# The sixth dense pass of a graph network, written as short inner loops of six matmuls

## What is computed

```python
edge_index = jnp.stack([src, dst])
x = _layernorm(x + L0(x))   # three layers of: t = x @ W.T + b; x = (t + segment_sum(t[src], dst)) / 2
x = _layernorm(x + L1(x))   # h = x @ W; segment_sum(norm * h[src], dst) + b
x = _layernorm(x + L2(x))   # the same with a PReLU
x = _layernorm(x + L3(x))   # per edge: z = silu(bn(Wg @ [x_src, x_dst])), softmax weights, segment_sum
```

## Time and profile before

| | |
|---|---|
| median of 3 runs | 7904.57 us |
| span of the profiled execution | 7903.8 us |
| TensorE matmul busy | 5452.6 us (69%), 34773 matmuls |
| VectorE busy | 3716.0 us (47%) |
| GpSimd busy | 1922.7 us (24%) |
| ScalarE busy | 1419.9 us (18%) |
| DMA, mean over the span | 121 GB/s |
| mean granted TensorE clock | 0.825 of 2.4 GHz |

### The profile page before, as it was taken

The page is one execution under the profiler, slowest core; times in us unless marked ns, Lnnn a source line. Parts: engine busy times, 40 slices in busy tenths (PEclk is TensorE's granted clock), DMA queues, the critical chain, the costliest instruction groups (busy, mean ns, idle before and its releaser), DMA issues.

```text
span 7903.8 us, 132209 instructions
## 1 busy us (share of the span) xinstructions
PE 5452.6 (69%) x34773; PEld 3268.0 (41%) x34774; DVE 3716.0 (47%) x12527; ACT 1419.9 (18%) x4414; POOL 1922.7 (24%) x3005
## 2 busy tenths in 40 slices
PE   5999999869999999999321211111115899888883
PEld 1333333346666666666100000000002588877773
DVE  8888888733223444455100000000001488888887
ACT  0111233200000000000000000000000176665552
POOL 1222122100000000000577767777774000000000
PEclk8999999879999999999655555555556999999997
DMA  1000111135565656555433333333336555444442
GB/s 40 33 41 41 65 76 78 65 110 191 185 194 187 194 184 194 184 187 182 140 107 107 113 107 109 107 108 108 109 103 146 154 138 129 123 119 114 110 111 59
DMA packets 305154, 958.44 MB, mean 121 GB/s; under 512 B 55676, under 2 KB 124888, under 8 KB 285929
## 3 DMA queue, kind: packets, MB, share of 16 engines
q1 hardware_dynamic: 238729, 741.78, 30.4%
q0 software_dynamic: 66400, 216.36, 10.2%
HBM read 765.85 MB, written 192.08 MB: 121 GB/s over the span
## 4 chain that ended last, share of the span: by engine, by line
PE 48%; another core or an unknown queue 21%; DVE 13%; issue 12%; DVEq 2%; ACT 2%; SPq 1%; DMA 1%; ACTq 0%; POOLq 0%; POOL 0%; PEld 0%; PEldq 0%
PE banks L678 28%; PE banks L637 12%; DVE HSf L1028 3%; PE banks L632 2%; PE banks L627 2%; DVE HSf L1024 1%; DVE HSf L1035 1%; PE banks L668 1%; DVE HSf L1005 1%; PE banks L731 1%; ACT HSf L563 1%; PE banks L738 1%; DVE HSf L1030 1%; ACT AB L518 1%
## 5 line engine op out<-in xcount | busy, mean ns | idle before, releaser
L678 PE MATMUL banks<-HSf,AB 128*128 128x384 bf16 (+2 forms) x14406 | 2727.3, 338 | 1812.8 <-issue 1786.7
L678 PEld LDWEIGHTS banks<-HSf,AB 128*128 128x128 bf16 x14406 | 1417.4, 99 | 3012.7 <-issue 2160.9
L474 POOL DMA_INDIRECT HSf<-table_d,IX x1600 | 1515.0, 947 | 644.0 <-issue 488.6
L903 DVE TENSOR_REDUCE US<-banks 128x128 f32<-128x384 f32 (+1 forms) x294 | 164.1, 558 | 2977.4 <-remote 1738.4
L861 DVE TENSOR_SCALAR T<-T 128x784 bf16<-128x784 f16 x2352 | 985.1, 419 | 224.2 <-PE banks L637 208.1
L637 PE MATMUL banks<-T 128*128 128x392 bf16 x4704 | 965.6, 337 | 3.7 <-DVE T L862 3.0
L637 PEld LDWEIGHTS banks<-T 128*128 128x128 bf16 x4704 | 378.3, 99 | 565.0 <-DVE T L862 380.6
L862 DVE TENSOR_SCALAR T<-T 128x128 bf16<-128x128 f16 x2352 | 581.6, 247 | 0.0
L563 ACT ACTIVATE HSf<-HSf 128x130 f32<-128x130 f32 x1808 | 575.5, 392 | 0.5 <-DVE HSf L1039 0.5
L462 POOL DMA_DIRECT2D table_d<-T x1 | 2.5, 2545 | 2241.1 <-DVE HSf L879 2241.1
L518 ACT ACTIVATE AB<-banks 128x392 f32 x784 | 347.1, 494 | 1102.4 <-PE banks L641 1102.4
(11 more groups left out here) (212 smaller groups left out, 3554.2 us busy)
## 6 DMA issues: line engine op xcount, KB each, us to landing
AB<-counts_d SPq DMA_DIRECT2D x294, 800.0 KB
AB<-counts_d SPq DMA_DIRECT2D x294, 768.0 KB
HSf<-rows_d SPq DMA_DIRECT2D x452, 260.0 KB, 3.1
rows_d<-HSf POOLq DMA_DIRECT2D x100, 1040.0 KB
counts_d<-AB SPq DMA_DIRECT2D x49, 1568.0 KB, 5.2
HSf<-dst_d SPq DMA_DIRECT2D x452, 128.0 KB, 3.4
HSf<-table_d,IX POOLq DMA_INDIRECT x1600
table_d<-T POOLq DMA_DIRECT2D x1, 3185.0 KB, 28.0
```

Source lines behind the costliest of these rows:

```text
L474: g.indirect_dma_start(GS[:, t, :], None, table_d, bass.IndirectOffsetOnAxis(ap=IX[:, t:t + 1], axis=0)).then_inc(g_in[k], 16)
L678: ins = pe.matmul(agg[par][:, 0:wide], AB[:, k, (s - HA * h) * P:(s - HA * h + 1) * P], HS[:, (q - 1) & 1, s, 0:wide], start=(s == 0), sto ...
```

## The change

Pass 6 is taken out of the common code. A block becomes `short(b, par, n)`: one matmul with fixed addresses, a loop of three turns with six matmuls each, six with fixed addresses; then for the second half six with fixed addresses, a loop of two turns with six matmuls each, and six with fixed addresses. In the inner loops the tile of counts and the row block of features are chosen by registers. Matmuls, their order, waits and increments are the same. The counting of `start` and `stop` is too: the first matmul starts the bank, the last one stops it.

```diff
+            def some(par, k, at, s0, last):
+                for t in range(6):
+                    if isinstance(s0, int):
+                        lhs, rhs = AB[:, k, (s0 + t - at) * P:(s0 + t - at + 1) * P], HS[:, 1, s0 + t, 0:387]
+                    else:
+                        lhs = AB[:, k, ds((s0 + t - at) * P, P)]
+                        rhs = HS[:, 1, ds(s0 + t, 1), 0:387].rearrange("p a f -> p (a f)")
+                    ins = pe.matmul(agg[par][:, 0:387], lhs, rhs, start=False, stop=(last and t == 5), skip_group_check=True)
+                return ins
+
+            def short(b, par, n):
+                if not isinstance(b, int):
+                    pe.wait_ge(agg_read, b + (5 * NB + 1))
+                pe.wait_ge(a_in[2 * par], n * 16 + 16)
+                pe.matmul(agg[par][:, 0:387], AB[:, 2 * par, 0:P], HS[:, 1, 0, 0:387], start=True, stop=False, skip_group_check=True)
+                with pe.Fori(0, 3) as c:
+                    some(par, 2 * par, 0, pe.snap(c * 6 + 1), False)
+                some(par, 2 * par, 0, 19, False).then_inc(a_used[par], 1)
+                pe.wait_ge(a_in[2 * par + 1], n * 16 + 16)
+                some(par, 2 * par + 1, HA, HA, False)
+                with pe.Fori(0, 2) as c:
+                    some(par, 2 * par + 1, HA, pe.snap(c * 6 + (HA + 6)), False)
+                some(par, 2 * par + 1, HA, 43, True).then_inc(agg_done, 1)
...
                 pe.wait_ge(h_ready, q * NB)
+                if q == 6:
+                    short(0, 0, m * 25)
+                    with pe.Fori(0, NB // 2) as i:
+                        short(pe.snap(i * 2 + 1), 1, i + m * 24)
+                        short(pe.snap(i * 2 + 2), 0, i + (m * 25 + 1))
+                    continue
                 mm(q, 0, 0, m * 25)
```

## The result

The changed kernel takes 7941.29 us, median of 5 runs (7925.89 to 7969.84), where the kernel before took 7905.13 us in the same comparison (5 runs). The ratio is 1.0052, with a 95% interval of 1.0039 to 1.0066: 31 to 52 us slower, 36 us by the medians. The forecast was 8013 us, +109. The sign and the range (7865 to 8165 us) held, the size was about three times too large.

The account below looks back on a forecast made before the run. TensorE's matmuls in pass 6 were taken as held back beside GpSimd's gathers; afterwards 26.3 blocks at 12.5 us, 329 us instead of 220, add 109 to 7903.8, giving 8013 us. Range 7865 to 8165 us.

Parts of the forecast that it names:

- What bounds the kernel: Pass 6: TensorE's already issued matmuls are held back while GpSimd gathers, 2.35 us each; instruction fetch is not the cause.
- the stretch: Pass 6, 3810 to 6045 us, beside GpSimd's 1600 gathers: 950 matmuls, 19.4 blocks, 115 us a block.
- In the gather stretch ... I cost it at nothing: Pass 6 beside the gathers: about 12 us of register work a block lies beside held-back matmuls and costs nothing.
- The cover of 103 us a block: Pass 6 beside the gathers: 115 us a block less about 12 us of register work leaves 103 us.
- Taken: per turn ... 2158 ns ... 12.6 us a block: Pass 6 after the gathers: sequencer time per six-matmul turn; five turns 10.8 us, setup 0.9, fixed pairs 0.9.
- the sum: Whole kernel: 26.3 remaining blocks at 12.5 us, 329 us instead of 220, +109 us, giving 8013 us; chance 0.48.
- Number of blocks: Pass 6 after the gathers: 49 - 3.3 - 19.4 = 26.3 blocks remain.
- The forecast's own lower end of 7908 us: Whole kernel: time if a block after the gathers takes 8.1 us; the upper end is 8092 us at 15.5 us.
- Clock: Rival, pass 6 after the gathers: TensorE's clock falls to half, 15.8 us a block, +196, 8100 us; chance 0.08.
- Relief by short loops: Rival, pass 6 beside gathers: repeated turns escape the hold-back; in part 7873 us (chance 0.08), altogether 7600 us (0.12).
- The branch: TensorE's inner loops: taken branch 208 ns by the trace; the skill's 108 ns would make the result about 13 us lower.
- Nothing happens: Rival, pass 6 after the gathers: register work at its lower bound, 5.8 us a block, is hidden; 7904 us, chance 0.06.

Follow-up runs that it names:

- base_2: Kernel before with an AND behind every register value loaded from memory, repeated beside a kernel before at 7906.34 us: 7951.00 us.
- changed_2: Changed pass 6 on the kernel before with the AND behind loaded register values: 8009.55 us, +59 us against base_2.
- thirteen_2: Pass 6 with thirteen turns of three matmuls a block, on the kernel before with the AND, run again: 8214.07 us, +263 us against base_2.
- thirteen_turns: Changed kernel plus the AND, with inner loops of three matmuls, thirteen turns a block instead of five: 6370.25 us, 14 us above base.
- few_after: Changed kernel with one gather issued of each set of sixteen, edge stage on rows not gathered: 5984.26 us.
- few_before: Kernel before with one gather issued of each set of sixteen, edge stage on rows not gathered: 5903.03 us.
- base: Kernel before with an AND behind every register value loaded from memory: 6356.63 us, beside the kernel before at 6299.42 us.
- addr_only: Against the changed kernel, plus the AND: the 30 matmuls a block unrolled without inner loops or branches, keeping register addresses: 6352.60 us.
- late_puts: Against base_2: GpSimd converts indices for 64 gathers at once, a round ahead, and issues each put one set later: 7939.21 us.

## Why the prediction was right or wrong

- **What bounds the kernel** was right for the case measured: the stretch, its end at the gathers' end and its 19.4 blocks all stayed (949 matmuls, forecast 950). That it was so exact is luck: base_2 had 1016 matmuls in its stretch, changed_2 1067. Taking the stretch as a property of the program was too simple: it exists in the held case alone.
- **"In the gather stretch ... I cost it at nothing"**: right for five turns. The cover of 103 us a block did its work; thirteen_2 shows where it ends.
- **"Taken: per turn ... 2158 ns ... 12.6 us a block"** is the step that failed, by the size of its terms; that the sequencer's time sets the pace was right. A turn takes 1.95 us, and a block 10.4. The long register instructions were put at 103 ns, the median of the window code, and none here is above 79: a matmul of the loop takes 255 ns where the sum has 303 (103 + 50 + two gaps + 50). Counter and branch with their gaps were put at 340 ns and cost 420. So five turns are 1.0 us shorter. The rest of a block, 0.9 us for loop setup and 0.9 us for the 19 fixed matmuls, takes 0.6: the sequencer passes twelve fixed pairs in some 0.2 us, not at 50 ns each. That is another 1.2 us. The excess over the hidden 8.1 us was put at 4.4 us and is 2.3: an error of 20% in the block became one of 90% in the cost.
- **Number of blocks**: 26.3 forecast, 1295 matmuls are 26.4. The forecast's own lower end of 7908 us is no result of its terms: 26.3 x 8.1 - 220 is -7, 7897 us. With 10.4 us the sum would have been 26.3 x 10.4 - 220 = +54 us, within the spread of the two comparisons (+36 and +59).
- **Clock** (forecast rival): excluded, 1.00 and 0.99 after the gathers, and in thirteen_turns 1.00 throughout pass 6.
- **Relief by short loops**: excluded. few_after against few_before and changed_2 against base_2 show a loss of 2.1 to 2.3 us a block and no gain. The Trainium skill (Runtime: NRT & Kernel Launch, Instruction fetch mechanics) has a taken branch stall when its target lies outside the fetched window. The body of 98 matmuls showed none: in base 2181 matmuls keep TensorE busy for all of the 360 us from 3830 to 4190, 8.1 us a block, its branches included.
- **The branch**: the trace has 207 ns where it is taken and 76 ns where it is not. The Trainium skill (Advanced Engine Details and Errata, Control Flow Timing) has about 108 ns; the measurement decides, and what a turn pays is more than either, 0.42 us: the branch with the counter and the restart around it.
- **Nothing happens** was the nearest rival by size. addr_only shows it would have been right for the address arithmetic alone.

The two medians (+36 and +59 us) differ by more than either spread explains well: changed runs scatter over 44 us in the first comparison and 15 in the second. Why is open.

## What to carry to other kernels

When a cost is the excess of one pace over another, compute the block first and then ask what the error of the block does to the excess; and take the price of an instruction on the sequencer from a row of its own kind: register work of another loop and a guess for a plain pair made the whole error here. A wait called "issue" on one engine may be made by another that only posts DMAs: compare the pace at which DMAs are issued with the pace at which they land (here 1.25 against 1.40 us), and try issuing them more slowly before rewriting the engine that waits. Eight small memsets in the gather loop saved 1090 us in the held case; the loop change cost 36 to 59 us there.

That version is only the better one where the hold-back exists: it beats both kernels there (6807 against 7894 us) and is 348 us slower than the kernel before where it does not.

## What was not expected of the hardware

- The same kernel takes 7891 to 7906 us or 6296 to 6299 us, from one comparison to the next, and the difference is whether TensorE's instructions are held back beside GpSimd's indirect DMAs. Both were seen on one and the same chip.
- In the held case indirect DMAs are served at 1.40 us each, twice 0.70; a register instruction that is held lasts 700 or 1400 ns (thirteen_2, and SP in the earlier trace rows), and late_puts' weight loads start 2.1, 2.8 or 3.5 us apart. Plain DMAs of the same engine, 539 in 405 us at 367 GB/s, hold nothing back.
- At 1.25 us between issues pass 6 takes 2497 us, at 1.39 us 514 and at 1.45 us 465; no held run lies between the first two. What is shared, and why it is so in some comparisons only, was not found.
